# A projection of attention tiles: one tile at a time with its own bias product, or two tiles together in one bank

## The reference, cut to what matters

```
xn = layernorm(x)
q, k, v = heads(xn @ wq.T + bq), heads(xn @ wk.T + bk), heads(xn @ wv.T + bv)   # 16 heads of 16
positions = clip(base + anchor + tanh(offsets(q)) * 6)       # 12 samples for each query and head
scores    = q . sample(k, positions) / 4 - rel_scale * |positions - base|
out       = sum over samples of softmax(scores) * sample(v, positions)
s = out @ wo.T + bo
g = silu(mixture of 8 experts, top 2, of xn)
result = x + s * g
```

## Time and profile before

| | us |
|---|---|
| median of 3 runs | 1453.27 (1451.84 to 1455.79) |
| the profiled execution | 1458.15, its span 1456.5 |

### The profile page before, as it was taken

How to read it: one execution, slowest core, us unless ns; L and a number is a source line. 1 busy time by engine, 2 the same in 40 slices (tenths; PEclk the granted TensorE clock), 3 DMA queues, 4 the chain that set the end, 5 groups by cost and what they waited for, 6 DMA issues and landing times. The chain is left out here.

```text
span 1456.5 us, 36103 instructions
## 1 busy us (share of the span) xinstructions
PE 1363.9 (94%) x13687; PEld 1092.2 (75%) x13688; DVE 1223.2 (84%) x1697; ACT 802.1 (55%) x1873; POOL 856.9 (59%) x566
## 2 busy tenths in 40 slices
PE   5998999996699999999999999999999989989988
PEld 4864566566588888878888888888888867777766
DVE  7846665644999899998998998999999899999951
ACT  2547677765454545545454545455544537666655
POOL 1000377775477888887877878887787843201121
PEclk9998899997899999999999999999999999999999
DMA  7942456776656786767686676768577759889998
GB/s 232 343 156 89 114 177 190 247 232 201 211 149 192 183 236 164 207 170 240 167 242 176 186 220 146 211 150 247 143 214 215 205 136 261 245 243 234 274 252 161
DMA packets 204251, 293.54 MB, mean 202 GB/s; under 512 B 25601, under 2 KB 161029, under 8 KB 203891
## 3 DMA queue, kind: packets, MB, share of 16 engines
q0 software_dynamic: 65792, 146.59, 39.2%
q1 hardware_dynamic: 110723, 133.04, 28.8%
q10 hardware_dynamic: 27632, 12.64, 3.4%
HBM read 182.83 MB, written 117.74 MB: 206 GB/s over the span
## 5 line engine op out<-in xcount | busy, mean ns | idle before, releaser
L1221 POOL DMA_INDIRECT moe_rows<-expert_mem,token_of x142 | 361.6, 2547 | 94.4 <-issue 46.5
L1498 PE MATMUL pA<-xsT,expert_mem 128*128 128x256 f32 x1136 | 261.9, 385 | 13.7 <-DMA expert_mem<-in_w_l 7.6
L1504 PE MATMUL pY<-expert_mem 128*128 x1136 | 264.2, 386 | 0.0
L1202 POOL DMA_INDIRECT expert_mem<-xn_rows,token_of x138 | 232.4, 1684 | 49.0 <-issue 45.6
L1498 PE MATMUL pB<-xsT,expert_mem 128*128 128x256 f32 x1136 | 256.8, 380 | 0.0
L1498 PEld LDWEIGHTS pA<-xsT,expert_mem 128*128 128x128 f32 x1136 | 218.9, 193 | 45.7 <-issue 10.8
L1504 PEld LDWEIGHTS pY<-expert_mem 128*128 128x128 f32 x1136 | 210.4, 190 | 41.3 <-issue 16.1
L1498 PEld LDWEIGHTS pB<-xsT,expert_mem 128*128 128x128 f32 x1136 | 216.3, 190 | 28.9
L1713 DVE SCALAR_TENSOR_TENSOR parts<-pos_pair,prob 128x768 f32<-128x768 f32 x224 | 197.5, 952 | 0.6
L1341 ACT ACTIVATE expert_mem<-pA,b1sel 128x256 f32<-128x256 f32 x284 | 111.0, 473 | 128.8 <-issue 124.9
L1350 ACT ACTIVATE expert_mem<-pB,b1sel 128x256 f32<-128x256 f32 x284 | 111.2, 475 | 111.0 <-PE pB L1498 111.0
(11 more groups left out here) (212 smaller groups left out, 2234.2 us busy)
## 6 DMA issues: line engine op xcount, KB each, us to landing
expert_mem<-in_w_l POOLq DMA_DIRECT2D x71, 1024.0 KB, 7.3
band<-band_rows SPq DMA_DIRECT2D x256, 96.0 KB, 4.4
S_rows<-expert_mem SPq DMA_DIRECT2D x64, 376.0 KB
band_rows<-wgt SPq DMA_DIRECT2D x12, 1536.0 KB, 7.2
pos_pair<-pos_rows SPq DMA_DIRECT2D x28, 384.0 KB, 5.6
xn_rows<-expert_mem SPq DMA_DIRECT2D x16, 512.0 KB, 5.6
v_rows<-expert_mem SPq DMA_DIRECT2D x16, 512.0 KB, 4.3
moe_rows<-zeros POOLq DMA_DIRECT2D x4, 2048.0 KB
```

Of the source, the lines that this page charges most:

```text
L1202: nc.gpsimd.indirect_dma_start(out=xs[:, u, s], out_offset=None, in_=dram["xn"], in_offset=bass.IndirectOffsetOnAxis(ap=keep["inv"][:, 2 * ...
L1221: nc.gpsimd.indirect_dma_start(out=dram["moe"], out_offset=bass.IndirectOffsetOnAxis(ap=keep["inv"][:, 2 * n + s:2 * n + s + 1], axis=0), ...
L1498: mm = nc.tensor.matmul(dst[:, c], w1[:, 1 - u, k, o * HID + c * P:o * HID + (c + 1) * P], xsT[:, k], start=(k == 0), stop=(k == KC - 1))
L1504: mm = nc.tensor.matmul(pY[:, s], hid[:, h, c, s * P:(s + 1) * P], w2[:, c, ds(e * D, D)], start=False, stop=(s == 1 and c == HC - 1))
```

## The change

Tiles 2g and 2g + 1 are projected together, as pair g. One bias product over 512 columns opens the whole bank (pY or pO, in turn), with the bias rows read twice; then come the four f32 products of the two tiles, each tile in its half. TensorE does this behind the value products of tile 2g + 2, so behind every second tile; behind the other tiles nothing stands between value products and the next transposes. The last pair follows the last tile's value products. ScalarE evacuates 512 columns at once, for even t. `outT` gets four slots in place of two and moves into the shared piece of SBUF, in front of `proj`, which goes from ten unit slots to nine. The semaphores `pj_done` and `pj_ready` now count pairs, and the waits on them are changed to match. Units of four tiles, their multiply and their stores stay.

```diff
-ROW_SLOTS = 10
+ROW_SLOTS = 9
+OUT_SLOTS = 4
...
-        pJ = [pY[:, 0], pO[:, 0]]
+        pJ = [pY, pO]
...
             def evacuate_out(t):
                 act.wait_ge(pv_done, t + 1)
-                if t >= 2:
-                    act.wait_ge(pj_done, t - 1)
+                if t >= OUT_SLOTS:
+                    act.wait_ge(pj_done, t // 2 - 1)
                 for c in range(KC):
-                    ins = nc.scalar.activation(outT[:, t % 2, c], pV[t % 2][:, c * P:(c + 1) * P], ACT.Identity, bias=bv[:, c:c + 1])
+                    ins = nc.scalar.activation(outT[:, t % OUT_SLOTS, c], pV[t % 2][:, c * P:(c + 1) * P], ACT.Identity, bias=bv[:, c:c + 1])
...
-                act.wait_ge(pj_done, t + 1)
+                act.wait_ge(pj_done, g + 1)
...
-                nc.scalar.activation(proj[:, k % ROW_SLOTS, t % GROUP], pJ[t % 2], ACT.Identity).then_inc(pj_ready, 1)
+                nc.scalar.activation(proj[:, k % ROW_SLOTS, t % GROUP:t % GROUP + 2], pJ[g % 2][:], ACT.Identity).then_inc(pj_ready, 1)
...
-                if t > 0:
-                    evacuate_proj(t - 1)
+                if t > 0 and t % 2 == 0:
+                    evacuate_proj(t // 2 - 1)
...
-            def project(t, u):
-                pe.wait_ge(outT_ready, t + 1)
-                if not (isinstance(t, int) and t < 2):
-                    pe.wait_ge(pj_ready, t - 1)
-                for c in range(KC):
-                    nc.tensor.matmul(pJ[u], outT[:, u, c], wo[:, c], start=(c == 0), stop=False)
-                nc.tensor.matmul(pJ[u], ones3[:], bo[:], start=False, stop=True).then_inc(pj_done, 1)
+            def project(g, t, u):
+                pe.wait_ge(outT_ready, t + 2)
+                if not (isinstance(g, int) and g < 2):
+                    pe.wait_ge(pj_ready, g - 1)
+                nc.tensor.matmul(pJ[u][:], ones3[:], bo[:].unsqueeze(1).broadcast_to([NB, 2, D]), start=True, stop=False)
+                for a in range(2):
+                    for c in range(KC):
+                        mm = nc.tensor.matmul(pJ[u][:, a], outT[:, 2 * u + a, c], wo[:, c], start=False, stop=(a == 1 and c == KC - 1))
+                mm.then_inc(pj_done, 1)
...
                     times_v(t, j, i)
-                    if not (first and j == 0):
-                        project(t - 1, (j + 1) % 2)
+                    if j == 2:
+                        project(i * 2, i * GROUP, 0)
+                    if j == 0 and not first:
+                        project(i * 2 - 1, i * GROUP - 2, 1)
...
-            project(TILES - 1, 1)
+            project(TILES // 2 - 1, TILES - 2, 1)
...
-                dve.wait_ge(pj_ready, (k + 1) * GROUP)
+                dve.wait_ge(pj_ready, (k + 1) * GROUP // 2)
...
-                dve.wait_ge(pj_ready, t + 1)
+                dve.wait_ge(pj_ready, t // 2 + 1)
```

More of the change, by code:

```diff
@@ L993, in sem @@
             return keep["sems"].enter_context(nc.semaphore(name))
-        UNIT_F, LATE_F = GROUP * D, 2 * SUBS * D
-        assert W2_F == MOE_SLOTS * UNIT_F and W1_F == 2 * LATE_F and W1_AT + LATE_F + ROW_SLOTS * UNIT_F <= SHARED_F
+        UNIT_F, LATE_F, OUT_F = GROUP * D, 2 * SUBS * D, OUT_SLOTS * KC * P
+        assert W2_F == MOE_SLOTS * UNIT_F and W1_F == 2 * LATE_F and W1_AT + LATE_F + OUT_F + ROW_SLOTS * UNIT_F <= SHARED_F
         shared, w2, w1, xs = keep["shared"], keep["w2"], keep["w1"], keep["xs"]
@@ L1003, in mix_block @@
         late_v = shared[:, W1_AT:W1_AT + LATE_F].rearrange("p (u s c) -> p u s c", u=2, s=SUBS)
-        proj = shared[:, W1_AT + LATE_F:W1_AT + LATE_F + ROW_SLOTS * UNIT_F].rearrange("p (k a c) -> p k a c", k=ROW_SLOTS, a=GROUP)
+        outT = shared[:, W1_AT + LATE_F:W1_AT + LATE_F + OUT_F].rearrange("p (u c n) -> p u c n", u=OUT_SLOTS, c=KC)
+        proj_at = W1_AT + LATE_F + OUT_F
+        proj = shared[:, proj_at:proj_at + ROW_SLOTS * UNIT_F].rearrange("p (k a c) -> p k a c", k=ROW_SLOTS, a=GROUP)
         wo = sb("wo", [P, KC, D])
@@ L1036, in mix_block @@
         v = sb("vk", [P, 2, SUBS, D])
-        outT = sb("outT", [P, 2, KC, P])
         pX = ps("pX", [P, KC, PAIR])
@@ L1381, in load_v, with evacuate_proj @@
                     act.dma_start(slot_v(f)[e:ROWS:2, :, e * HALF:(e + 1) * HALF], keys_of(n, e)).then_inc(v_loaded[f], 16)
-            def evacuate_proj(t):
+            def evacuate_proj(g):
+                t = 2 * g
                 k = t // GROUP
-                act.wait_ge(pj_done, t + 1)
+                act.wait_ge(pj_done, g + 1)
                 if k == ROW_SLOTS - 2 and t % GROUP == 0:
```

## The result

The changed kernel takes **1464.4 us** (median of 12 runs, 1456.1 to 1470.3), the kernel before beside it 1455.8 (12 runs, 1451.8 to 1459.5): ratio **1.0058**, interval 1.0041 to 1.0075. It is slower by about 8.5 us (6 to 11); the forecast was 1448.8. The profiled execution took 1466.48 us with a span of 1464.9, so it stands 2.1 above its median.

The account below looks back on a forecast made before the run. TensorE was taken to set the last stage's pace, except when waiting for band transfers. 12.8 - 1.2 - 0.8 - 6.6 + 1.0 - 0.7 = 4.5 us less, from the median 1453.27 to 1448.8 us; range 1443 to 1455.5.

Parts of the forecast that it names:

- the two pairs behind the first gate: Last stage, after tile 7: two pairs run into bands issued between 1218 and 1227, losing 0.8 us.
- The clock, 1.0 us back: After the long wait ending at 1413.76: a shorter gap before it gives back between 0 and 3 us, 1.0 taken.
- rival "slower": Late transfers hit odd tiles in nine stretches, 1.7 us each: 5.2 us more, 1458.5 us; chance 0.13.
- ScalarE's copies, "it costs nothing": Even tiles: the pass ends 0.2 us later, band evacuation queues behind it, but its value products come a full tile later.
- Tile 5's gate: ScalarE's gate waits for expert rows until 1222.09, unmoved, holding tile 7's value products; 1.2 us saved until then is lost.
- TensorE's 12.8 us less: Projections in the last stage: 2.14 us a pair against 2.54, 0.40 us less for each of 32 pairs.
- the engine that sets the pace, as long as data comes in time: Last stage: TensorE, busy 234 of 252 us, sets the pace whenever data comes in time.
- The spacing, 6 x 1.1 us: Band transfers: odd tiles get 6.5 us from issue to use, even 8.7; six late stretches lose 6.6 us.
- parity is chance: Late band transfers: whether an odd or even tile is hit is chance; given as an argument against rival "slower".
- Late next: ScalarE's sixteenth exponential: if ScalarE is there over 2.5 us earlier, it stands, with the band evacuations behind it.
- The end: Tiles 62 and 63 projected together: their pass, multiply and stores come later, 0.7 us more.
- The stage's excess over 64 quiet tiles: Last stage: its time over 64 quiet tiles, 25 us before, should grow to some 34 over 64 x 3.34 us.

Follow-up runs that it names:

- e1_place: Changed kernel, pairs still behind every second tile, but with the old products and a bias product for each tile: 1465.4 us against 1454.4, ratio 1.0088.
- e7_no_bias: Kernel before without the projection's bias products (output lacks the bias): 1451.1 us against 1452.0, ratio 0.9989.
- e3_early: Changed kernel with band transfers issued behind the transposes of four tiles earlier instead of the value products: 1447.4 us, ratio 0.9959 to the kernel before.
- e2_split: Changed kernel with one bias product and ScalarE pass a pair, but each tile's four products behind the next tile's value products: 1454.3 us against 1454.4, ratio 1.0004.
- e4_before_early: Kernel before with band transfers issued behind the transposes of four tiles earlier instead of the value products: 1446.2 us against 1454.4, ratio 0.9950.
- e12_best: Changed kernel with products split per tile, band transfers issued behind transposes, gates at 7 and 10, last exponential at tile 44: 1438.6 us against 1450.8, ratio 0.9924.
- e5_early_exp: Changed kernel with band transfers issued behind transposes and the last exponential at tile 44 instead of 42: 1444.1 us against 1452.0, ratio 0.9938.

## Why the prediction was wrong

The forecast was 4.5 us less, the measurement 8.5 us more. Term by term, forecast against the two profiled executions (us, minus is faster):

| term | forecast | measured |
|---|---|---|
| TensorE's work | -12.8 | some -12.8 |
| waits for bands (spacing 6.6, the two pairs behind the first gate 0.8) | +7.4 | +8.6 |
| waits for ScalarE's copy of the band (gate of tile 5) | +1.2 | +5.0 |
| the clock | -1.0 | about +10 |
| the end, to the issue of the last store | +0.7 | +1.3 |
| start of the stage | 0 | -6.8 |

- **The clock, 1.0 us back**: this is the step that failed. The prediction looked at one long wait and took the clock as a gain. Time at half clock went from 27.3 to 54.6 us. In the kernel before, a tile at half clock takes 5.4 us instead of 3.5; after, the way from an odd tile's transposes over the pair projection to the next even tile's takes 7.2 instead of 4.4. So the added time at half clock costs about 10 us, an estimate from these. The clock falls after waits that are not long: behind the one of 2.60 us at 1334.21 it is at half from 1334.9 on, behind one of 1.56 us at 1276.3 from 1276.8 on, and around the one of 4.66 us that ends at 1422.58 from 1420.2 on. The prediction's rival "slower" had the condition, "further if a grown gap lets the clock fall where it did not", without a price.
- **ScalarE's copies, "it costs nothing"**: the second term that was off. Behind tile 22 ScalarE's list has a gate and a preparation in front of the copy of tile 24's band. From the start of the projection's copy, ahead of these, to tile 24's value products ScalarE needs 5.5 us before and 5.7 after. TensorE is ready for them 4.4 us after that start before, and 3.2 after, since no projection stands behind tile 23 any more. So the wait grows from 1.09 to 2.43 us; the other traces with pairs have 2.2 to 2.5 there. The rows, before and then after:
```profile
1296.03 1.29 PE L1532 MATMUL pB<-bandT,vk 96*32 96x32 f32 x64 [1.09 <-ACT bandT L1366]
```
```profile
1295.91 1.28 PE L1535 MATMUL pB<-bandT,vk 96*32 96x32 f32 x64 [2.43 <-ACT bandT L1368]
```
- **Tile 5's gate**: 1.2 us were forecast. TensorE waited 2.47 us before tile 7's value products (0.16 before), as the gate waited 5.0 us for expert rows instead of 0.75. How much of that belongs to this one execution is open; these waits differ between traces (6.2 us in all here, 2.7 in e1_place).
- **TensorE's 12.8 us less**: the size was right (0.39 us a pair by the projections, 0.45 by the medians of two tiles, 0.34 to 0.40 in the other traces with pairs; 0.30 in the one quiet stretch, where transposes straight behind value products start some 0.1 us later). It was entered as time because 234 busy us of 252 were read as "the engine that sets the pace, as long as data comes in time". e7_no_bias and the table above say that here it goes into waits and half clock.
- **The spacing, 6 x 1.1 us**: its mechanism held, and its size nearly did: waits for bands grew by 8.6 us, and the distance was 6.8 us where 6.5 was forecast. Wrong was that parity is chance: where lateness spans two tiles or more the even one has slack and the odd one pays, 22.1 us on ten odd tiles against 0.9 on two even ones. The rival "slower, by the odd tile's wait" had the place and gave 1458.5; it came nearest, and it had 0.13.
- **Late next**: the prediction named a ScalarE that comes too early. In e3_early this happened; in the changed kernel the reverse did. TensorE late makes ScalarE late, so the exponential whose scores are ready at 1357.54 starts at 1374.65; VectorE stands 17.0 us for it (2.4 before). Its last weights begin 213.3 us after the stage did, 197.5 before, and the last burst of stores is that much later.
- **The end**: from the end of tile 63's value products to the issue of the last store it is 5.4 us instead of 4.1. The pair itself was priced well (the pass 0.60 us, 0.59 forecast). Not seen was that its bias product also waits 0.74 us for the output of tile 63.

The measured terms add up to about +5. Another 0.7 us is a wait at the stage's start, and 0.8 lie behind the last store's issue. The spans differ by 8.4; the rest is not accounted for. How the waits and the clock share the loss can't be told more closely: they come together in every run. The start of the stage, 6.8 us earlier, was in no term; without it the changed kernel would have been slower still.

That the place of the projections is the cause is shown from both sides (e1_place, e2_split). That a part of it acts through the bands' time to land is shown by e3_early, which gives the changed form about twice what e4_before_early gives that of before. The rest, waits for ScalarE and half clock that pairing keeps with early transfers too, is seen in the traces and was not isolated, and neither was the loop through VectorE.

The stage's excess over 64 quiet tiles was forecast at some 34 us and is near 47 (264.3 less 64 x 3.39).

Open is why pairing has more time at half clock in each of these pairs of traces, even where nothing waits for a band, and how much of the time in e12_best each kind of transfer holds.

## What to carry over

Before work is taken from the busiest engine, take for each of its regular waits the time from issue to use and the time from issue to landing; where they are near each other, the engine's saving is handed to the transfer. Some 4 to 5 us more of distance gave the kernel before 7 us here, and 23 us less of work gave it about 1. Work that sits between a buffer's release and its next use is also its slack: bunching it shortened the distance of every second buffer from 8.2 to 6.6 us, and the mean says little, for the shorter distance decides. A wait is to be priced with the slow clock that follows it. Release a buffer at its last reader; here that one line gave about 7 us before and 14 us after.

## What the runs showed of the hardware

Band transfers of 96 KB that land in 2.6 us in quiet stretches take 6.2 to 9.8 in the bursts (and 6.2 to 8.2 in the chain after), and value rows of 96 KB took 13.5 and 15.5 us in e5_early_exp. In a burst issuing stretches too; the chain of the kernel after:
```profile
1411.09 1.62 SPq L1172
...
1412.76 2.35 SPq L1172
...
1415.15 7.29 DMA band<-band_rows
...
1422.58 1.94 PE pA L1520 x8
1424.52 1.26 PE pB L1535 x55
1425.78 0.53 PE pO L1544
1426.31 3.71 PE pO L1547 x8
```
An issue that takes 0.59 us elsewhere took 1.62 and 2.35, which put the last transfer of the tile 2.8 us later. TensorE had waited 4.66 us, and the transposes behind it took 1.94 us instead of 1.11 and the products 3.71 instead of 1.92, at the lower of the two clock levels. Waits much shorter than this one were followed by the lower level too (1.56 us, at 1276.3), and others were not (1.22 us, at 1358.2).

The Trainium skill ("TensorE: Matmul & The Clock Gate", section "Step-by-step: what each phase is for") has the next weight load pulled ahead of products in flight, where their row groups don't conflict or it goes to the background weight buffer. By that rule alone the pair, with the same columns, would save nothing. The trace has 2.15 us against 2.54, so one bias product less, with its weight load and its switch from f32 to bf16 and back, is worth 0.39 us; which of these costs it is not separated.
